# Edge attributes of a graph network brought in feature by edge instead of turned on TensorE

## The chip, the cores and the metric

The kernel runs on one core of one Trainium2 chip. The metric is the device time of one execution, in microseconds (us), on random inputs of fixed shapes.

## The reference

Three layers of a relational graph network on 6250 nodes of 256 features and 100000 edges, sorted by their target node. Each edge has a source, a target, one of three types and 32 attributes. The result is added to the input and normalised.

```python
ew = edge_attr @ edge_w + edge_b                     # (100000, 256)
inv_cnt[i] = 1 / max(edges of type i per target, 1)
for l in range(3):
    msg = relu(x[src] * ew)
    out = x @ roots[l] + biases[l]
    for i in range(3):
        h = segment_sum(msg * (edge_type == i)[:, None], dst) * inv_cnt[i][:, None]
        out = out + h @ weights[l, i]
    x = x + relu(out)
return layernorm(x_input + x)
```

## The kernel before

The edges are cut into 782 tiles of 128, and four tiles make a group, 196 of them (the last has two tiles). In each of the three layers all tiles are worked through two by two. Such a pair is a step, q = 0 to 390. Every engine has its own written-out program, a loop over layers and steps in which q says what is issued when; engines meet only at semaphores. The program is one long straight line behind a check of the input (`both`, `fast`), with a general way beside it that these inputs do not take.

What a pair of tiles needs, engine by engine:

- GpSimd (POOL) issues a `gather` for each tile (line 692, an indirect DMA at line 700): 128 rows of x by the tile's sources, into one of twelve slots of `xg`. A gather waits until the sums of the tile that had its slot are done (`s_sc`).
- TensorE computes `edge_weights` (line 853): attributes times `edge_w` plus `edge_b`, for two tiles into a bank `pE`, with two of them. The left operand is `at`, 128 partitions by 512 edges, three slots (`TR`). Its partitions 0 to 31 hold the attributes' high part, 32 to 63 the low part that was left by rounding, and 64 and up are ones; so one product has both parts and the bias.
- VectorE multiplies the gathered rows by the edge weights in place (line 1300), adds earlier sums to the accumulator `acc` (`add_sums`, line 1138), and makes the matrices `S` that select target and type (line 1097).
- ScalarE applies the ReLU in place (line 791), and in layer 0 makes the one-hot matrices `oh_a` for counting (line 812).
- TensorE sums the messages by target and type, `collect` (line 888, matmuls at line 911), and in layer 0 the counts (line 903).
- When all edges of a block of 128 nodes are summed, the block is mixed: x is turned (`turn_x`), four products with the weights (`mix`, line 961), and VectorE forms the new x in five operations. The blocks start at steps that `plan` works out, six to twelve steps apart.

The part around the change is how `at` comes about. In layer 0, for each group g:

- SP issues `load_attr(g)`: 4 x 128 edges of 32 attributes each, edge by partition, 64 KB, into the slot g % 3 of `hs`, columns 32 to 63 of each tile.
- ScalarE's `high(g)` (line 745) writes the rounded attributes beside them, columns 0 to 31.
- VectorE's `split(g)` (line 1012) subtracts these from the raw ones in place: what is left is the low part.
- TensorE's `attr_turn(g)` (line 846) turns four tiles of 128 edges by 64 columns into the bank `pT`. This bank is shared with `turn_x`.
- ScalarE's `attr_copy(g)` (line 753) copies `pT` to `at`. It waits for the turn, for the edge products that still read the slot (`s_e`), and for the slot's store (`s_ao`).
- SP's `keep_attr(g)` stores the 64 x 512 values of `at` to DRAM (`attr_t`, 128 KB). In layers 1 and 2 SP only loads them back (`reload_attr`).

The places in the steps: SP issues the load of group q/2 + 4 and right behind it the store of group q/2, at even q. ScalarE copies group (q+2)/2 and rounds group (q+6)/2 at even q, after the ReLU. At odd q VectorE splits group (q+6)/2 and TensorE turns group (q+3)/2. SP's load of group g waits until group g - 3 has been turned:

```python
if g >= 3:
    eng.wait_ge(s_tr, g - 2)
```

SP's queue also carries the loads and stores of blocks, in order with the rest. A table `brow` of the first target of each tile, read into VectorE's registers at line 1274, lies in a buffer of its own.

## Time and profile before

| | |
|---|---|
| median of 3 timed runs | 2969.16 us (2966.05 to 2969.5) |
| the profiled execution, first to last instruction | 3581.6 us |
| TensorE: matmuls, weight loads | busy 79%, 73% |
| VectorE, ScalarE, GpSimd | busy 60%, 36%, 62% |
| DMA | 465.42 MB, mean 130 GB/s |

The profiled execution has no time of its own besides its span; what lies around the span is not shown. It is 612 us longer than the timed median. Busy is the time in which an engine had an instruction running; waits for semaphores, register loads and branches are not in it. The chain that ended last is followed back from the last instruction, and the page gives its shares of the span: TensorE 59%, waits for nothing that is shown 17%, VectorE 9%, ScalarE 4%. Within TensorE's share the sums (line 911) have 29%, the edge products (line 867) 14%, the mixes (line 961) 12% and the turns of the attributes (line 846) 2%.

### The profile page before, as it was taken

The numbers are of one execution on the slowest core, as the hardware profiler recorded it, in microseconds if no ns is written. First come the engines' busy times: TensorE is split into PE (matmuls) and PEld (weight loads), VectorE is DVE, ScalarE is ACT, GpSimd is POOL, SyncE is SP. The second block draws the span as 40 slices with busy tenths as digits, with TensorE's granted clock in tenths as the row PEclk, the third lists the DMA queues.
The fourth block names the chain that finished last, engine by engine and source line by source line (L and its number), as shares of the span: only waits on it lengthen the run. The fifth ranks groups of instructions, "written<-read, shape, count | busy, mean of one in ns | idle before, by whom it ended". The sixth has DMA issues, their size and how long they took to land.

```text
span 3581.6 us, 59909 instructions
## 1 busy us (share of the span) xinstructions
PE 2843.8 (79%) x18436; PEld 2613.2 (73%) x18436; DVE 2148.4 (60%) x6028; ACT 1289.4 (36%) x2738; POOL 2224.3 (62%) x2364
## 2 busy tenths in 40 slices
PE   6888888888888877787777877777777777787777
PEld 6777777777777777777777777767777777776776
DVE  5666666666666555555555555555556656665665
ACT  5555555555555322222222222222222222222222
POOL 6666666666666566666666666656666666666664
PEclk9999999999999888888898889988888888899898
DMA  6554555555455444444444444444444444444443
GB/s 148 135 137 132 137 135 138 136 137 137 131 137 145 133 120 127 125 130 127 126 127 127 134 124 127 131 127 132 126 124 128 125 127 131 125 130 124 128 128 99
DMA packets 334989, 465.42 MB, mean 130 GB/s; under 512 B 158995, under 2 KB 221646, under 8 KB 334670
## 3 DMA queue, kind: packets, MB, share of 16 engines
q0 software_dynamic: 112608, 307.65, 30.1%
q1 hardware_dynamic: 221244, 153.70, 15.6%
q8 instruction: 156, 2.56, 0.3%
q14 instruction: 163, 1.34, 0.1%
q10 hardware_dynamic: 818, 0.18, 0.0%
HBM read 403.94 MB, written 57.36 MB: 129 GB/s over the span
## 4 chain that ended last, share of the span: by engine, by line
PE 59%; issue 17%; DVE 9%; another core or an unknown queue 8%; ACT 4%; DVEq 2%; DMA 0%; ACTq 0%
PE bank L911 29%; PE bank L867 14%; PE bank L961 12%; DVE acc L1138 4%; PE bank L846 2%; DVE xg L1300 1%; ACT oh_a L812 1%; DVE t L1155 1%; ACT at L753 1%; DVEq L1274 1%; PE bank L936 1%; DVEq L1138 1%; ACT xg L791 1%; DVE S L1097 1%
## 5 line engine op out<-in xcount | busy, mean ns | idle before, releaser
L700 POOL DMA_INDIRECT xg<-x,idx x1540 | 1457.0, 946 | 870.6 <-issue 351.7
L911 PE MATMUL bank<-S,xg 128*128 128x96 f32 x9384 | 1450.5, 304 | 360.3 <-issue 176.3
L911 PEld LDWEIGHTS bank<-S,xg 128*128 128x128 f32 x9384 | 1313.6, 216 | 429.2 <-issue 385.4
L791 ACT ACTIVATE xg<-xg 128x512 f32<-128x512 f32 x1170 | 736.7, 630 | 2102.3 <-DVE xg L1300 1193.8
L1300 DVE TENSOR_TENSOR xg<-xg,bank 128x512 f32<-128x512 f32 x1170 | 800.8, 684 | 691.0 <-remote 329.4
L1138 DVE TENSOR_TENSOR acc<-acc,bank 128x192 f32 x2346 | 816.7, 348 | 570.0 <-PE bank L911 343.0
L867 PE MATMUL bank<-wsb,at 128*128 128x256 f32 x4692 | 985.7, 337 | 213.6 <-issue 123.3
L700 POOL DMA_INDIRECT xg<-in_x_dram,idx x782 | 742.2, 949 | 454.2 <-PE bank L911 211.2
L867 PEld LDWEIGHTS bank<-wsb,at 128*128 128x128 f32 x4692 | 749.3, 214 | 297.6 <-issue 195.9
L961 PE MATMUL bank<-W,acc 128*128 128x256 f32 (+1 forms) x1764 | 515.9, 415 | 7.2 <-issue 6.4
L961 PEld LDWEIGHTS bank<-W,acc 128*128 128x128 f32 (+1 forms) x1764 | 386.9, 258 | 17.3 <-issue 12.1
L1097 DVE TENSOR_TENSOR S<-bank,kr 128x384 f32<-128x384 f32 x588 | 323.2, 550 | 0.8 <-issue 0.7
L812 ACT ACTIVATE oh_a<-iota,lo 128x128 bf16<-128x128 bf16 x782 | 266.2, 389 | 3.5 <-PE bank L911 3.4
L1155 DVE SCALAR_TENSOR_TENSOR t<-bank,inv,t 128x256 f32<-128x256 f32 (+1 forms) x441 | 209.2, 474 | 17.6 <-remote 10.1
L961 PE MATMUL bank<-W,xT 128*128 128x256 f32 (+1 forms) x588 | 200.2, 472 | 0.9 <-issue 0.8
L846 PE MATMUL bank<-ident,hs 128*64 128x128 f32 x782 | 131.3, 295 | 32.5 <-issue 19.2
L961 PEld LDWEIGHTS bank<-W,xT 128*128 128x128 f32 (+1 forms) x588 | 127.9, 238 | 17.3 <-issue 3.0
L903 PE MATMUL bank<-oh_b,oh_a 128*128 128x12 bf16 x782 | 81.2, 175 | 68.2 <-issue 62.5
L753 ACT ACTIVATE at<-bank 64x512 fp32r<-64x512 f32 x196 | 113.3, 578 | 44.1 <-remote 25.8
L1251 DVE TENSOR_TENSOR cnt<-cnt,bank 128x12 f32<-128x12 f32 x391 | 60.7, 155 | 104.7 <-remote 97.0
L903 PEld LDWEIGHTS bank<-oh_b,oh_a 128*128 128x128 bf16 x782 | 52.6, 107 | 95.5 <-issue 75.3
L846 PEld LDWEIGHTS bank<-ident,hs 128*64 128x64 f32 x782 | 93.2, 128 | 39.4 <-issue 35.1
(75 smaller groups left out, 789.7 us busy)
## 6 DMA issues: line engine op xcount, KB each, us to landing
at<-attr_t SPq DMA_DIRECT2D x390, 128.0 KB
attr_t<-at SPq DMA_DIRECT2D x195, 128.0 KB
xg<-x,idx POOLq DMA_INDIRECT x1540
xg<-in_x_dram,idx POOLq DMA_INDIRECT x782
hs<-in_edge_attr_dram SPq DMA_DIRECT2D x194, 64.0 KB
x<-t SPq DMA_DIRECT2D x96, 128.0 KB
xblk<-x SPq DMA_DIRECT2D x96, 128.0 KB
y<-t SPq DMA_DIRECT2D x94, 128.0 KB
```

The lines of the kernel that those rows point to most:

```text
L700: eng.indirect_dma_start(out=xg[:, n % XR, :], out_offset=None, in_=rows_in, in_offset=bass.IndirectOffsetOnAxis(ap=rows_at, axis=0)).then ...
L753: eng.activation(at[0:64, g % TR, 0:w], pT[0:64, 0:w], ACT.Copy).then_inc(s_atc, 1)
L791: eng.activation(v, v, ACT.Relu).then_inc(s_r, 1)
L812: eng.activation(oh_a[:, j % AR, :], iota[:, 1:129], ACT.Sign, bias=lo[:, tile(j):tile(j) + 1]).then_inc(s_oh, 1)
L846: last = eng.transpose(pT[0:64, 128 * i:128 * i + 128], hs[:, g % 3, i, :], ident[:, :])
L867: last = eng.matmul(pE[Q % 2][:, 256 * i:256 * i + 256], at[:, sl, c:c + 128], wsb[:, p, :], start=(p == 0), stop=(p == 1))
L911: last = eng.matmul(sums_bank(l, q, i)[:, 192 * i + 96 * h:192 * i + 96 * h + 96], xg[:, n % XR, 128 * h:128 * h + 128], S[:, slot(l, 2 * ...
L961: last = eng.matmul(o, a, W[:, 2 * (r % 4) + h, :], start=(h == 0), stop=(h == 1))
L1097: eng.tensor_tensor(S[:, at4:at4 + w, :], steps_of[:, 1:WK + 1].unsqueeze(1).to_broadcast([128, w, WK]), kr[:, c:c + w].unsqueeze(2).to_br ...
L1138: eng.tensor_tensor(a, a, sums_bank(l, q, i)[:, 192 * i:192 * i + 192] .rearrange("p (h w) -> p h w", h=2), ALU.add).then_inc(s_acc, 1)
L1155: return eng.scalar_tensor_tensor(tt, products(k, m), inv[0:n, 3 * blocks[k] + r:3 * blocks[k] + r + 1], tt, ALU.mult, ALU.add)
L1300: eng.tensor_tensor(v, v, pE[Q % 2][:, :].rearrange("p (i d) -> p i d", i=2), ALU.mult).then_inc(s_m, 1)
```

## The change

The host hands over a further array, `attr_2`: the attributes feature by edge, 32 rows, written twice one above the other, so 64 x 100096 values. SP loads 64 x 512 of it for a group, 128 KB, into one of two slots of `hs` (`HR2`). ScalarE copies all 64 partitions with rounding straight to `at`, and VectorE replaces partitions 32 to 63 of `at` by the raw values less the rounded ones. TensorE takes no part, and `attr_turn` and `attr_copy` are gone. The store to DRAM and the layers 1 and 2 stay as they are. The steps of the remaining work move: ScalarE does group (q+4)/2 at even q, and VectorE group (q+3)/2 at odd q. SP's load of group g waits for the split of group g - 2, and its store of group g for that group's split. `brow` moves to the partitions 64 to 127 of `hs`.

```diff
+    HR2 = 2
-    BR = 196
+    BR = 392
-        hs = sb("hs", [128, 3, 4, 64])
+        hs = sb("hs", [128, HR2, 512])
-        brow = sb("brow", [128, BR], I32)
+        brow = hs[64:128, :, :].rearrange("p a b -> p (a b)")[:, 0:BR].bitcast(I32)
...
             def load_attr(g):
-                if g >= 3:
-                    eng.wait_ge(s_tr, g - 2)
-                a, n = 128 * head_tile(order[g]), tiles_of(g) - (g == short)
...
-                eng.dma_start(hs[:, g % 3, 0:n, 32:64], edge_attr[a:a + 128 * n, :]
-                              .rearrange("(j p) d -> p j d", p=128)).then_inc(s_an[g % 3], 16)
+                if g >= HR2:
+                    eng.wait_ge(s_lo, g - HR2 + 1)
+                a, w = 128 * head_tile(order[g]), 128 * tiles_of(g)
+                eng.dma_start(hs[0:64, g % HR2, 0:w], attr_2[:, a:a + w]).then_inc(s_an[g % HR2], 16)
 
             def keep_attr(g):
                 w = 128 * tiles_of(g)
-                eng.wait_ge(s_atc, g + 1)
+                eng.wait_ge(s_lo, g + 1)
                 eng.dma_start(attr_t[g, :, 0:w], at[0:64, g % TR, 0:w].bitcast(F32)).then_inc(s_ao[g % TR], 16)
...
             load_attr(1)
-            load_attr(2)
...
-                            if 3 <= q // 2 + 4 < NG:
+                            if HR2 <= q // 2 + 4 < NG:
                                 load_attr(q // 2 + 4)
...
             def high(g):
 
-                eng.wait_ge(s_an[g % 3], attrs(g))
-                eng.activation(hs[:, g % 3, :, 0:32].bitcast(F32R), hs[:, g % 3, :, 32:64], ACT.Copy).then_inc(s_hi, 1)
-
-            def attr_copy(g):
                 w = 128 * tiles_of(g)
-                eng.wait_ge(s_tr, g + 1)
+                eng.wait_ge(s_an[g % HR2], 16 * (g // HR2 + 1))
                 if g >= TR:
                     eng.wait_ge(s_e, 2 * (g - TR + 1))
                     eng.wait_ge(s_ao[g % TR], 16 * (g // TR))
-                eng.activation(at[0:64, g % TR, 0:w], pT[0:64, 0:w], ACT.Copy).then_inc(s_atc, 1)
+                eng.activation(at[0:64, g % TR, 0:w], hs[0:64, g % HR2, 0:w], ACT.Copy).then_inc(s_hi, 1)
...
-                        if l == 0 and q % 2 == 0 and 1 <= (q + 2) // 2 < NG:
-                            attr_copy((q + 2) // 2)
+                        if l == 0 and q % 2 == 0 and 1 <= (q + 4) // 2 < NG:
+                            high((q + 4) // 2)
...
-                        if l == 0 and q % 2 == 0 and 1 <= (q + 6) // 2 < NG:
-                            high((q + 6) // 2)
...
-                        if l == 0 and q % 2 and 1 <= (q + 3) // 2 < NG:
-                            attr_turn((q + 3) // 2)
...
             def split(g):
 
-                raw, high = hs[:, g % 3, :, 32:64], hs[:, g % 3, :, 0:32]
+                w = 128 * tiles_of(g)
                 eng.wait_ge(s_hi, g + 1)
-                eng.tensor_tensor(raw, raw, high, ALU.subtract).then_inc(s_lo, 1)
+                eng.tensor_tensor(at[32:64, g % TR, 0:w], hs[32:64, g % HR2, 0:w],
+                                  at[32:64, g % TR, 0:w].bitcast(F32), ALU.subtract).then_inc(s_lo, 1)
...
-                        if l == 0 and q % 2 and 1 <= (q + 6) // 2 < NG:
-                            split((q + 6) // 2)
+                        if l == 0 and q % 2 and 1 <= (q + 3) // 2 < NG:
+                            split((q + 3) // 2)
```

How the change stands in the engines' programs, at one place of layer 0 each. SP's queue, before (`s_tr` is the turn, `s_atc` the copy out of the bank, `s_rd` a block's last operation on VectorE):

```order
L562 DMA hs<-in_edge_attr_dram 128x4x32 [waits s_tr]
L568 DMA attr_t<-at 64x512 [waits s_atc]
L562 DMA hs<-in_edge_attr_dram 128x4x32 [waits s_tr]
L568 DMA attr_t<-at 64x512 [waits s_atc]
L562 DMA hs<-in_edge_attr_dram 128x4x32 [waits s_tr]
L568 DMA attr_t<-at 64x512 [waits s_atc]
L580 DMA xblk<-in_x_dram 128x256 [waits s_rd]
```

and in the change, where `s_lo` is the split:

```order
L554 DMA hs<-in_attr_dram 64x512 [waits s_lo]
L559 DMA attr_t<-at 64x512 [waits s_lo]
L554 DMA hs<-in_attr_dram 64x512 [waits s_lo]
L559 DMA attr_t<-at 64x512 [waits s_lo]
L554 DMA hs<-in_attr_dram 64x512 [waits s_lo]
L559 DMA attr_t<-at 64x512 [waits s_lo]
L571 DMA xblk<-in_x_dram 128x256 [waits s_rd]
```

The order of SP's transfers is the same; the load and the store both wait for VectorE's split now.

ScalarE, before (`s_ao0` is the landing of a store to `attr_t`, `s_an` of a load of attributes, `s_m` the multiplication):

```order
L791 ACTIVATE xg<-xg 128x512 [waits s_m]
L812 ACTIVATE oh_a<-iota,lo 128x128 [waits s_sc] x2
L791 ACTIVATE xg<-xg 128x512 [waits s_m]
L753 ACTIVATE at<-bank 64x512 [waits s_ao0,s_e,s_tr]
L745 ACTIVATE hs<-hs 128x4x32 [waits s_an2]
L812 ACTIVATE oh_a<-iota,lo 128x128 [waits s_sc] x2
L791 ACTIVATE xg<-xg 128x512 [waits s_m]
L812 ACTIVATE oh_a<-iota,lo 128x128 [waits s_sc] x2
```

and in the change (line 775 is the ReLU, 794 the one-hots):

```order
L775 ACTIVATE xg<-xg 128x512 [waits s_m]
L794 ACTIVATE oh_a<-iota,lo 128x128 [waits s_sc] x2
L775 ACTIVATE xg<-xg 128x512 [waits s_m]
L738 ACTIVATE at<-hs 64x512 [waits s_ao0,s_e,s_an0]
L794 ACTIVATE oh_a<-iota,lo 128x128 [waits s_sc] x2
L775 ACTIVATE xg<-xg 128x512 [waits s_m]
L794 ACTIVATE oh_a<-iota,lo 128x128 [waits s_sc] x2
```

Two operations for a group have become one, which waits for the landed load and the landed store together.

TensorE around the turn of a block of x (line 936 before, 904 in the change), before:

```order
L936 MATMUL bank<-ident,xblk 128x128 x2
L867 MATMUL bank<-wsb,at 128x256 x4
L903 MATMUL bank<-oh_b,oh_a 128x12 x2
L911 MATMUL bank<-S,xg 128x96 x4
L846 MATMUL bank<-ident,hs 64x128 x4
L867 MATMUL bank<-wsb,at 128x256 x4
L903 MATMUL bank<-oh_b,oh_a 128x12 x2
L911 MATMUL bank<-S,xg 128x96 x4
L961 MATMUL bank<-W,xT 128x256 x2
```

and in the change:

```order
L904 MATMUL bank<-ident,xblk 128x128 x2
L838 MATMUL bank<-wsb,at 128x256 x4
L874 MATMUL bank<-oh_b,oh_a 128x12 x2
L882 MATMUL bank<-S,xg 128x96 x4
L838 MATMUL bank<-wsb,at 128x256 x4
L874 MATMUL bank<-oh_b,oh_a 128x12 x2
L882 MATMUL bank<-S,xg 128x96 x4
L927 MATMUL bank<-W,xT 128x256 x2
```

The turns of the attributes (line 846) are gone, and nothing stands in their place.

## Rows read from the trace of the kernel before

**Rows 1.** Spans by core: span, mean granted clock of TensorE

```profile
core 0: 3581.6 us, clock 0.896
```

**Rows 2.** Groups by line: names, count | busy us, mean ns | idle before, releasers

```profile
L700 POOL DMA_INDIRECT xg<-x,idx x1540 | 1457.0, 946 | 870.6 <-issue 351.7 <-PE bank L911 291.8 <-remote 227.2
```

**Rows 3.** Waits of POOL: us in total, times, longest us

```profile
POOL xg L700 <- issue: 527.0, 1722, 0.6
POOL xg L700 <- PE bank L911: 505.4, 436, 10.0
POOL xg L700 <- remote: 302.9, 186, 2.0
```

**Rows 4.** Timeline of POOL: start us, us, engine, line, operation [idle before, releaser]

```profile
4.73 1.10 POOL L700 DMA_INDIRECT xg<-in_x_dram,idx  x1 [0.97 <-DMA idx<-in_src_t_dram]
...
22.46 0.95 POOL L700 DMA_INDIRECT xg<-in_x_dram,idx  x1 [2.55 <-PE bank L911]
...
1211.05 0.94 POOL L700 DMA_INDIRECT xg<-y,idx  x1 [1.84 <-remote]
...
1217.30 0.95 POOL L700 DMA_INDIRECT xg<-y,idx  x1 [0.30 <-issue]
1228.27 0.94 POOL L700 DMA_INDIRECT xg<-x,idx  x1 [10.02 <-PE bank L911]
...
2405.89 0.94 POOL L700 DMA_INDIRECT xg<-x,idx  x1 [8.76 <-PE bank L911]
...
3561.22 0.95 POOL L700 DMA_INDIRECT xg<-x,idx  x1 [0.30 <-issue]
```

**Rows 5.** Layers 0, 1: us, busy us of PE, PEld, DVE, ACT, POOL, clock, DMA share

```profile
20.00:1200.00 1180.00, 981.71 (x7138) 891.00 (x7137) 750.12 (x2470) 675.16 (x1676) 730.23 (x770) 0.93 0.51 137
1240.00:2395.00 1155.00, 904.94 (x5486) 839.73 (x5486) 654.84 (x1597) 294.71 (x483) 729.26 (x773) 0.87 0.44 128
```

**Rows 6.** Timeline of TensorE's weight loads, layer 0

```profile
1168.35 0.59 PEld L867 LDWEIGHTS bank<-wsb,at 128*128 128x128 f32 x4
...
1169.92 0.94 PEld L961 LDWEIGHTS bank<-W,acc 128*128 128x128 f32 x4
...
1176.73 0.44 PEld L846 LDWEIGHTS bank<-ident,hs 128*64 128x64 f32 x4
```

**Rows 7.** Groups by line that the change takes away or replaces

```profile
L846 PE MATMUL bank<-ident,hs 128*64 128x128 f32 x782 | 131.3, 295 | 32.5 <-issue 19.2 <-DVE hs L1012 7.0 <-ACT xT L799 6.3
...
L753 ACT ACTIVATE at<-bank 64x512 fp32r<-64x512 f32 x196 | 113.3, 578 | 44.1 <-remote 25.8 <-PE bank L846 14.2 <-issue 2.3
...
L745 ACT ACTIVATE hs<-hs 128x128 fp32r<-128x128 f32 x196 | 58.0, 296 | 0.0
L1012 DVE TENSOR_TENSOR hs<-hs 128x128 f32<-128x128 f32 x196 | 55.7, 285 | 4.4 <-ACT hs L745 3.4 <-issue 1.1
```

**Rows 8.** Groups by line nearest to the new operations

```profile
L1300 DVE TENSOR_TENSOR xg<-xg,bank 128x512 f32<-128x512 f32 x1170 | 800.8, 684 | 691.0 <-remote 329.4 <-PE bank L867 247.9 <-issue 110.1
...
L791 ACT ACTIVATE xg<-xg 128x512 f32<-128x512 f32 x1170 | 736.7, 630 | 2102.3 <-DVE xg L1300 1193.8 <-issue 907.3
```

**Rows 9.** Timeline of VectorE: two steps of layer 0 without a wait

```profile
714.70 0.69 DVE L1300 TENSOR_TENSOR xg<-xg,bank 128x512 f32<-128x512 f32 x1 [0.38 <-issue]
...
718.75 0.68 DVE L1300 TENSOR_TENSOR xg<-xg,bank 128x512 f32<-128x512 f32 x1
```

**Rows 10.** Timeline of SP's queue: the load and the store of one group

```profile
701.62 0.37 SPq L562 DMA_DIRECT2D hs<-in_edge_attr_dram  x1
702.04 0.51 SPq L568 DMA_DIRECT2D attr_t<-at  x1
```

**Rows 11.** DMA issues: name, engine, count, KB, us from issue to landing

```profile
acc<-in_dst_t_dram SPq DMA_DIRECT2D x1, 391.0 KB, 3.9
...
idx<-in_src_t_dram ACTq DMA_DIRECT2D x1, 4.0 KB, 2.0
idx<-in_src_t_dram ACTq DMA_DIRECT2D x1, 2.0 KB, 3.2
```

45 lines of the change are left out of this document (13 added, 32 removed).

## The prediction

> **What bounds the kernel now.** I first read the span against the timed runs. The profiled execution lasted 3581.6 us [rows 1], the timed runs 2969.16 us in the median: the profiled one is 612 us, or 21%, longer, so its times cannot be added up as they stand. What can be used of it is how long each thing takes when nothing disturbs it. TensorE has the largest busy share of the page, and the chain that ended last runs mostly through it; taken alone, that says that removing its work pays.
>
> The waits of POOL say otherwise. POOL issues 2346 gathers, each 0.946 us [rows 2]. In 1722 of the gaps between them it waited for nothing the profile shows, 0.306 us each (527.0 / 1722) [rows 3]; five gaps in a row put the pitch at (1217.30 - 1211.05) / 5 = 1.25 us [rows 4]. That is a floor for the program. Add it up: first gather at 4.7 us; 2345 pitches of 1.25 us, 2931; the 13th gather, the first behind the branch, waits 2.55 - 0.30 = 2.2 us more; the two turns from layer to layer 10.02 - 0.30 = 9.7 and 8.76 - 0.30 = 8.5 us; from the last gather to the end 3581.6 - 3561.2 = 20.4 us [rows 1, 4]. Sum: 2977 us. The timed median is 8 us (0.3%) below it; a pitch of 1.2467 us, 0.946 + 0.30 with the rounding of the rows, would give it exactly. A second count from the same views: the waits for TensorE and for landings are 505.4 + 302.9 us in 622 gaps; with 0.306 us left in each of them, 3581.6 - 808.3 + 190.3 = 2964 us, and 2984 with the 20 us of the branch and the two turns put back [rows 1, 3]. So the profiled execution is long because of interruptions that the timed ones do not have, and the timed kernel is POOL issuing gathers with hardly a hole. Two tiles are one step, so a step is 2.50 us and a group of four tiles, which one attribute load serves, 5.0 us.
>
> The other engines have to stay under that pace. Layer 0 and layer 1 do, at nearly one pace, 1180 us for 770 gathers against 1155 us for 773, although TensorE is busy 982 us in the one and 905 us in the other [rows 5].
>
> **The change part by part.**
> *TensorE loses the turns.* Four transposes a group, 0.44 us of weight loads at the full clock [rows 6]; times 196 groups that is 86 us (all of the group row: 131.3 us busy [rows 7]). A step of the edge products, counts and sums takes 1169.92 - 1168.35 = 1.57 us, half a turn 0.22, and a block's four mixes of 0.9 us every 8 steps 0.45: 2.24 us, and 2.39 us where blocks follow every 6 steps [rows 6]. Both are under 2.50, which hides them. Worth: nothing to at most 86 us. I take nothing, because the floor above already accounts for the whole time.
>
> *ScalarE* did a copy out of PSUM, 578 ns, and a rounding, 296 ns [rows 7]. It now does one copy of 64x512 from SBUF; the nearest row is the 128x512 ReLU at 630 ns [rows 8]. Saved: 0.24 us a group, 48 us in all, of an engine busy 675 of 1180 us [rows 5]. Hidden, worth nothing.
>
> *VectorE* subtracted 128x128 in 285 ns [rows 7] and now 32x512: time goes by elements along a partition, so the 128x512 row counts, 684 ns [rows 8]. That is 0.40 us more a group, 78 us in all. Two steps without a wait, with block work and the register load in them, take 718.75 - 714.70 = 4.05 us [rows 9]; plus 0.40 is 4.45, still under 5.0. Cost nothing, with 0.55 us of cover left; before it had 0.95.
>
> *SyncE and the two rings.* Loads grow from 64 to 128 KB, 12.8 MB in all. The DMA engines' share is 0.51 in layer 0 and 0.44 in layer 1 [rows 5], so that is no bound. But the order of waits changes. Before, SP's load for group g+4 waited for the turn of group g+1, and the store of group g behind it came five steps ahead of the copy that overwrites its slot. Now the load of g+4 waits for the split of g+2, at VectorE's step 2g+1; the store of g queues behind it; and ScalarE's copy for g+3, at its step 2g+2, needs that store landed. Behind it wait the one-hots of the next step, the next ReLU, and VectorE's split of g+3, which again frees SP. One round of this loop: the store starts 702.04 - 701.62 = 0.42 us behind the load [rows 10]; the landing L; the copy 0.63; the split 0.68; and 0.2 us for the four hops (estimate: 0.03 to 0.1 each by the starts in the timelines). The trace shows no landing of such a store. The nearest rows are 2.0 and 3.2 us for 4 and 2 KB and 3.9 us for 391 KB [rows 11]; 128 KB lies nearest the small ones, on the line from 2.0 to 3.9 at 2.6 us. The round is 1.93 + L = 4.5 us against 5.0: it fits. At the ends it is 3.9 and 5.8 us. I take 4.5 us, cost nothing. ScalarE will be seen waiting at this copy all the same, up to about 1 us a group, since it reaches it some 2 us after the split; it waited 44.1 us there in all before [rows 7]. The Trainium skill ("DMA: Bandwidth & Descriptors", Anatomy of one DMA) gives 2.0 us plus bytes by 436 GB/s for a DMA that GpSimd issues; by it L would be 2.3 and the round 4.2 us, and the sum stays.
>
> *The start.* No turn stands ahead of the first sums; they may come 1 us earlier, and the 13th gather with them [rows 4]. Bounds 0 and 2.2 us; taken 1. The branch behind the check stays.
>
> Sum: 2969.2 - 1 = **2968 us**. The ring of twelve gathers is six steps deep, 15 us, so a late copy now and then does not reach POOL. (A measurement of this kernel can tell about 0.2%, 6 us, from no change.)
>
> **Rivals.**
> *TensorE shares the bound in layer 0.* For it: at the granted 0.93 [rows 5] the dense step is 2.39 / 0.93 = 2.57 us, over 2.50. Layer 0 takes 1.532 us a gather and layer 1 1.494: times 782 that is 30 us more. If half goes to the turns (the counts are the rest), 15 us come back: 2953 us. Against it: without interruptions TensorE has no reason to sit at the lower clock, and the floor leaves no such 30 us. Should the timed pitch be well under 1.25, all 86 us could count, 2883 us; I hold that for very unlikely.
>
> *The store loop becomes the bound, slower.* It decides from L = 3.07 us on, where a round passes 5.0. At the 3.2 us of the 2 KB row it is 5.13 us, 0.13 x 196 = 25 us: 2993 us; at 3.9 us it would be 0.83 x 196 = 163 us. For it: the store now runs behind a load of 128 KB on the same queue, among gathers, and VectorE has half the cover that it had. Against it: the larger of these landings are from the start, where many loads are issued together.
>
> *POOL is held up by the new subtraction, slower.* The split reads two SBUF operands, as the old one did, and 0.40 us longer. If POOL stood still meanwhile, 78 us would be added: 3046 us. Against it: POOL's gathers take 0.946 us in layers 1 and 2 [rows 2], which have no split, and 0.95 us in layer 0 as well [rows 4]. The Trainium skill ("SBUF — State Buffer", SBUF: two separate sides) says that a VectorE operation with two SBUF inputs and a GpSimd operation that reads SBUF lock each other out of shared ports.
>
> *The change does not do what it says*: the turns are gone from TensorE's program, so I give this none.
>
> **How the numbers follow.** POOL paces as before 0.57; TensorE's relief shows 0.20; store loop 0.18; ports 0.05. Faster by over 0.2% 0.20, within 0.57, slower 0.23. The likeliest case gives 2968 us. The range must leave out no more than 0.2: down to 2948 (the relief at 20 us), up to 2998 (the loop at 3.2 us of landing, and a little), leaving out the 86 us, L above 3.2 us and the ports.
>
> **What would show it.** In the changed profile: the pitch of POOL's gathers again 1.25 us; TensorE's busy time in layer 0 down by 90 to 130 us while the layer keeps its length; the split at 0.68 to 0.70 us; ScalarE's copy near 0.63 us, with idle time before it, released by a landing, over the 44.1 us of before but under 200. A median under 2955 us would prove me wrong on TensorE. One over 2980 us with ScalarE idle over 1.5 us before each copy would say that the store loop binds; with gathers longer than 0.95 us, the ports.

## The result, and the profile after

| | before | changed |
|---|---|---|
| median of 4 timed runs each | 2967.91 us | 3016.82 us |
| lowest to highest | 2966.05 to 2969.5 | 3013.34 to 3022.49 |
| the profiled execution, span | | 3011.4 us |

The changed kernel is slower by 48.9 us, ratio 1.017, 95% interval 1.0156 to 1.0184. The forecast was 2968 us with a range up to 2998.

The page of the changed kernel (span; busy time by engine; TensorE's granted clock; the chain that ended last, by engine and by line):

```profile
span 3011.4 us, 57947 instructions
...
PE 2562.5 (85%) x17654; PEld 2355.0 (78%) x17654; DVE 2222.4 (74%) x6028; ACT 1247.4 (41%) x2542; POOL 2236.1 (74%) x2363
...
PEclk9899899999999999999999999999999999999999
...
PE 32%; DMA 30%; POOL 12%; issue 10%; DVE 8%; ACT 4%; SPq 3%; DVEq 0%; ACTq 0%; POOLq 0%
PE bank L882 17%; DMA attr_t<-at 16%; DMA xg<-x,idx 14%; POOL xg L689 12%; PE bank L927 8%; PE bank L838 7%; DVE at L976 3%; ACT at L738 3%; SPq L554 2%; DVE acc L1103 2%; DVE xg L1265 1%; DVE t L1120 1%; PE bank L904 0%; DMA at<-attr_t 0%; PE bank L874 0%
```

The granted clock stands at nine tenths or more in all but three of the 40 slices, and its mean is 0.952: 2.4 GHz for some nine tenths of the time, 1.2 GHz for the rest. TensorE is the busiest engine. The chain has an entry that the chain before did not show: the store `attr_t<-at`, 16% of the whole span, although it exists in one layer of three.

Groups of instructions (busy us, mean ns of one | idle us before them and what ended it):

```profile
L689 POOL DMA_INDIRECT xg<-in_x_dram,idx x782 | 753.4, 963 | 278.6 <-issue 163.5
...
L976 DVE TENSOR_TENSOR at<-hs,at 32x512 fp32r<-32x512 f32 x196 | 133.6, 682 | 172.4 <-ACT at L738 171.4
L738 ACT ACTIVATE at<-hs 64x512 fp32r<-64x512 f32 x196 | 123.3, 629 | 308.5 <-DMA attr_t<-at 278.1
```

ScalarE's copy is 629 ns and VectorE's split 682 ns, as forecast. The third row is where the forecast fell: 278.1 us of ScalarE's idle time end with the landing of a store. The first one holds the second surprise, 963 ns for a gather in layer 0.

The waits (engine, line, waited for: us in total, times, longest):

```profile
POOL xg L689 <- issue: 491.0, 1611, 0.5
ACT at L738 <- DMA attr_t<-at: 278.1, 174, 5.0
...
POOL xg L689 <- PE bank L882: 266.5, 734, 3.8
...
DVE at L976 <- ACT at L738: 171.4, 176, 4.2
```

The time goes on from ScalarE to VectorE (171.4 us). For POOL the waits of a profiled execution of the kernel before that took 2963.9 us (`before_again`, below) stand beside them:

```profile
POOL xg L700 <- issue: 498.8, 1635, 0.5
...
POOL xg L700 <- PE bank L911: 220.1, 710, 2.7
```

A stretch of layer 0 and one of layer 1 (busy us and count of PE, PEld, DVE, ACT, POOL; clock, DMA share, GB/s), first of the changed kernel, then of `before_again`:

```profile
20.00:980.00 960.00, 809.18 (x6031) 756.86 (x6030) 781.99 (x2337) 604.97 (x1406) 703.27 (x731) 0.94 0.59 171
1060.00:2000.00 940.00, 813.99 (x5410) 737.04 (x5409) 642.39 (x1572) 287.35 (x475) 710.90 (x753) 0.97 0.53 154
```

```profile
20.00:980.00 960.00, 891.11 (x7123) 845.30 (x7123) 746.04 (x2464) 666.00 (x1671) 725.62 (x765) 0.98 0.63 167
1010.00:1980.00 970.00, 834.98 (x5543) 753.06 (x5543) 659.59 (x1612) 293.91 (x486) 733.79 (x776) 0.97 0.53 153
```

In layer 1 the kernels go at one pace: 940 / 753 = 1.248 us a gather against 970 / 776 = 1.250. The loss is in layer 0: 731 gathers in 960 us against 765, that is 1.3133 us against 1.2549, and 0.0584 x 782 = 46 of the 49 us. The stretches are of one length but hold different amounts of work, so for busy times the whole of layer 0 is compared, from the first of its 782 gathers to the last (changed kernel, then `before_again`):

```profile
5.05:1035.60 1030.55, 860.05 (x6385) 803.65 (x6385) 839.04 (x2503) 649.65 (x1499) 753.35 (x782) 0.94 0.60 172
```

```profile
4.29:987.10 982.81, 903.27 (x7198) 855.53 (x7198) 760.96 (x2511) 682.71 (x1700) 743.41 (x782) 0.98 0.63 167
```

The layer is 48 us longer. TensorE had its relief (860 us busy against 903) and it bought nothing.

One thing on reading the times. The profile shown ahead of the prediction (span 3581.6 us) was no accident of one execution. The later half of the experiments ran on chips on which the kernel before takes 3584 to 3587 us run after run, as in the trace of [rows 3, 5]. Such traces have waits that end by "remote", a releaser that the profile can't name (302.9 us of POOL's in [rows 3]; the 2964-us trace has none above). They also hold fewer of the marks with which a DMA reports its landing, 3.8 for a gather in the mean where `before_again` has 15.8; so "remote" may be no more than marks that are missing, and landings are timed below from traces of the 2966-us chips alone. Why those chips are slower is open. Where an experiment ran there, the text says so, and its time is set only beside that of the kernel before on the same chip.

### The profile page after: what moved, and what is told of

The parts are those of the page before. It is cut to its first block, busy times and chain, and to the rows that moved or that the text cites. A ratio compares the mean times of both kernels' runs of the same rounds, so it can differ in the third digit from the quotient of the medians.

```text
span 3011.4 us, 57947 instructions
## 1 busy us (share of the span) xinstructions
PE 2562.5 (85%) x17654; PEld 2355.0 (78%) x17654; DVE 2222.4 (74%) x6028; ACT 1247.4 (41%) x2542; POOL 2236.1 (74%) x2363
## 4 chain that ended last, share of the span: by engine, by line
PE 32%; DMA 30%; POOL 12%; issue 10%; DVE 8%; ACT 4%; SPq 3%; DVEq 0%; ACTq 0%; POOLq 0%
PE bank L882 17%; DMA attr_t<-at 16%; DMA xg<-x,idx 14%; POOL xg L689 12%; PE bank L927 8%; PE bank L838 7%; DVE at L976 3%; ACT at L738 3%; SPq L554 2%; DVE acc L1103 2%; DVE xg L1265 1%; DVE t L1120 1%; PE bank L904 0%; DMA at<-attr_t 0%; PE bank L874 0%
## 5 line engine op out<-in xcount | busy, mean ns | idle before, releaser
L882 PE MATMUL bank<-S,xg 128*128 128x96 f32 x9384 | 1344.9, 289 | 126.9 <-DVE acc L1103 87.1
L882 PEld LDWEIGHTS bank<-S,xg 128*128 128x128 f32 x9384 | 1207.2, 201 | 201.1 <-ACT xg L775 154.5
L838 PE MATMUL bank<-wsb,at 128*128 128x256 f32 x4692 | 925.3, 321 | 149.2 <-DVE xg L1265 133.1
L838 PEld LDWEIGHTS bank<-wsb,at 128*128 128x128 f32 x4692 | 696.8, 199 | 220.4 <-issue 106.0
L976 DVE TENSOR_TENSOR at<-hs,at 32x512 fp32r<-32x512 f32 x196 | 133.6, 682 | 172.4 <-ACT at L738 171.4
L738 ACT ACTIVATE at<-hs 64x512 fp32r<-64x512 f32 x196 | 123.3, 629 | 308.5 <-DMA attr_t<-at 278.1
L927 PE MATMUL bank<-W,xT 128*128 128x256 f32 (+1 forms) x588 | 168.1, 412 | 0.0
L927 PEld LDWEIGHTS bank<-W,xT 128*128 128x128 f32 (+1 forms) x588 | 110.7, 206 | 10.5
L747 ACT ACTIVATE acc<-zcol 128x768 f32<-128x768 f32 (+1 forms) x98 | 81.2, 831 | 10.7 <-PE bank L927 10.7
L1132 DVE TENSOR_TENSOR t<-bank,bias 128x256 f32<-128x256 f32 (+1 forms) x147 | 61.1, 416 | 5.2 <-PE bank L927 4.7
```

The costliest lines, as they stand in the source:

```text
L738: eng.activation(at[0:64, g % TR, 0:w], hs[0:64, g % HR2, 0:w], ACT.Copy).then_inc(s_hi, 1)
L838: last = eng.matmul(pE[Q % 2][:, 256 * i:256 * i + 256], at[:, sl, c:c + 128], wsb[:, p, :], start=(p == 0), stop=(p == 1))
L882: last = eng.matmul(sums_bank(l, q, i)[:, 192 * i + 96 * h:192 * i + 96 * h + 96], xg[:, n % XR, 128 * h:128 * h + 128], S[:, slot(l, 2 * ...
L927: last = eng.matmul(o, a, W[:, 2 * (r % 4) + h, :], start=(h == 0), stop=(h == 1))
L976: eng.tensor_tensor(at[32:64, g % TR, 0:w], hs[32:64, g % HR2, 0:w], at[32:64, g % TR, 0:w].bitcast(F32), ALU.subtract).then_inc(s_lo, 1)
```

## The experiments

My theory after the result had two parts: **the store's round**, split, load, store, landing, copy, split, longer than the 5.0 us of a group; and, once the first runs were in, **the ports**: gathers drawn out by the longer split. The rivals were VectorE at its limit, and DMA traffic. The ports are a name for one thing that the runs show: a gather gets longer when it starts inside a VectorE operation that reads two operands from SBUF.

A table carries the readings from the chips on which the kernel before took 2966.3 and 2966.1 us (2967.9 beside the changed kernel). The pace is 960 us by the number of gathers in the stretch from 20 to 980 us, and the gather's mean is from the group rows of the same stretch (shown below, kernel by kernel). "Longer" is (mean - 950 ns) x 782, "holes" is what is left of (pace - 1.2549) x 782; one gather more or less in the count is 1.3 us, one ns 0.8 us. The two columns say where POOL's time went. They are not two prices that could be saved one by one: while POOL waits for the store's round anyway, a longer gather only fills a part of that wait.

| kernel | gathers | mean ns | pace us | longer us | holes us | sum us | timed over before us |
|---|---|---|---|---|---|---|---|
| before_again | 765 | 950 | 1.2549 | 0 | 0 | 0 | 0 |
| one_turn | 763 | 949 | 1.2582 | -1 | 3 | 3 | 1 |
| late_store | 757 | 949 | 1.2682 | -1 | 11 | 10 | 8 |
| changed | 731 | 963 | 1.3133 | 10 | 36 | 46 | 49 |
| store_first | 754 | 969 | 1.2732 | 15 | -1 | 14 | 17 |
| store_same_wait | 739 | 991 | 1.2991 | 32 | 3 | 35 | 31 |
| store_first_dve | 749 | 975 | 1.2817 | 20 | 1 | 21 | 22 |
| store_first_half | 765 | 951 | 1.2549 | 1 | -1 | 0 | 3 |
| store_first_wide | 751 | 971 | 1.2783 | 16 | 2 | 18 | 16 |

**before_again**, the kernel before, unchanged.

> The kernel before, unchanged, profiled once more: is its span of 3581.6 us, 612 us over the timed runs, a property of the kernel or of that one execution? If POOL paces it as summed up, an undisturbed profile spans 2960 to 2975 us, with POOL's gathers 1.25 us apart nearly everywhere.

Measured 2965.61 us, span 2963.9, clock 0.964. Its gathers in layer 0:

```profile
L700 POOL DMA_INDIRECT xg<-in_x_dram,idx x765 | 726.5, 950 | 234.5 <-issue 162.1 <-PE bank L911 72.4
```

It is the yardstick of the table. It has no long waits in POOL's row (2.7 us at most), and its pace is the floor of 1.25 us a gather that the prediction built from gaps [rows 3, 4].

**one_turn**: the kernel before with one of four turns, so without most of what the change takes from TensorE.

```diff
-                for i in range(tiles_of(g)):
+                for i in range(tiles_of(g) if g == 0 else 1):
```

> The kernel before with one of the four transposes of a group (from the second group on), so three quarters of the turn's TensorE work are left out (the attributes of three tiles of four are then stale ones), everything else as it was. If POOL paces the kernel: 2964 to 2970 us. If TensorE shares the bound in layer 0: up to 65 us less (three quarters of 86), 2903 to 2955 us.

Measured 2967.0 us, ratio 1.0002 (0.9993 to 1.0012).

```profile
L700 POOL DMA_INDIRECT xg<-in_x_dram,idx x763 | 724.4, 949 | 235.6 <-issue 167.0 <-PE bank L911 68.6
```

TensorE's relief alone is worth nothing: the interval bars a gain of over 0.1%. POOL starts its gathers at the same pace.

**store_first**: the changed kernel with SP's store ahead of its load.

```diff
-                            if HR2 <= q // 2 + 4 < NG:
-                                load_attr(q // 2 + 4)
                             if 0 <= q // 2 < NG:
                                 keep_attr(q // 2)
+                            if HR2 <= q // 2 + 4 < NG:
+                                load_attr(q // 2 + 4)
```

> The changed kernel with SyncE's store of group q/2 issued ahead of the load of group q/2+4, so that the store no longer stands behind the load's wait for the split of group q/2+2 and goes out two steps earlier. Store loop theory: ScalarE's idle time before its copy (309 us) falls below 60 us, POOL issues without a hole in layer 0 too, 2960 to 2975 us. If VectorE's longer subtraction or the DMA traffic is what costs, nothing changes: 3010 to 3020 us.

Measured 2982.89 us, ratio 1.0059 (1.0042 to 1.0076). ScalarE's wait for the store in layer 0 is next to nothing:

```profile
ACT at L738 <- DMA attr_t<-at: 6.7, 4, 2.9
```

```profile
L689 POOL DMA_INDIRECT xg<-in_x_dram,idx x754 | 730.9, 969 | 229.8 <-issue 156.6 <-PE bank L882 73.2
```

The load of group g+4 waits for the split of g+2 as before, but what follows it on the queue is now the store of g+1, not of g. Each store goes out a group earlier, the round is open, and 32 of the 49 us are back with two lines exchanged, although the store takes no less to land (3.25 us in the median) and the DMA share is as high as in before_again, 0.62 against 0.63. DMA traffic is out as the cause. I had expected 2975 us at most: 17 us stay though ScalarE no longer waits. The gathers show where: 969 ns.

**store_same_wait**: store first again, but held until the split for which the load waits. It keeps the round and takes only the load from in front of the store.

```diff
                             if 0 <= q // 2 < NG:
+                                eng.wait_ge(s_lo, min(q // 2 + 3, NG))
                                 keep_attr(q // 2)
```

> The changed kernel with the store ahead of the load, but made to wait for the split of group q/2+2 all the same. Only the 0.5 us behind the load's issue, and the load's bytes ahead of it, are taken from the loop. Store loop theory: the round of 5.0 us becomes 4.2 to 4.5 us and the time 2970 to 2990 us. If what counts is how early the store goes relative to its split, whatever stands before it: about 3015 us. VectorE or traffic: 3015 us.

Measured 2996.82 us, ratio 1.0099 (1.0082 to 1.0116).

```profile
L690 POOL DMA_INDIRECT xg<-in_x_dram,idx x739 | 732.3, 991 | 228.2 <-issue 151.4 <-PE bank L883 76.8
```

ScalarE's wait for the store is 45.7 us in the stretch, against 259.1 us in the changed kernel, and POOL's holes are gone. The time is over store_first's and over my 2990 us all the same, and it is the gathers: 991 ns, the longest of all. That was the pointer to the second part of the theory. In this order 100 gathers start 0.05 to 0.5 us into a split, against 56 in store_first and 40 in the changed kernel, and every one of them is long.

**late_store**: the kernel before, its short split and its 64 KB loads, with each store held until a later split.

```diff
-                            if 0 <= q // 2 < NG:
-                                keep_attr(q // 2)
+                            if 0 <= q // 2 - 1 < NG - 1:
+                                eng.wait_ge(s_lo, min(q // 2 + 4, NG))
+                                keep_attr(q // 2 - 1)
...
```

> The kernel before, turns and all, with one thing changed: the store of a group is held until VectorE has split the group four further on, which leaves it one step before the copy that overwrites its slot, as in the changed kernel. Store loop theory: 2990 to 3030 us, with ScalarE waiting for a landing before the copy out of the bank. If the new subtraction, the larger loads or the missing turns are the cause: 2968 us.

Measured 2974.19 us, ratio 1.0025 (1.0015 to 1.0036), far under what I expected.

```profile
ACT at L756 <- DMA attr_t<-at: 54.1, 99, 3.2
```

```profile
L703 POOL DMA_INDIRECT xg<-in_x_dram,idx x757 | 718.5, 949 | 241.9 <-issue 156.9 <-PE bank L914 85.0
```

ScalarE waits for the store 99 times, 54.1 us in the stretch, and 8 us reach the end. A miss of mine: I had looked at how late one store is. What counts is the length of the closed round. Here it is shorter than in the changed kernel, which also has the load's 0.52 us and a longer split in it, and whose store takes 3.05 us to land in the median against 2.49 here.

**store_first_dve**: store_first with one subtraction of VectorE's more for each group, 128x256, two SBUF operands.

```diff
+                if g >= 2:
+                    eng.wait_ge(s_pad, g - 2)
+                    eng.tensor_tensor(pad[:, :], wsb[:, 0, :].bitcast(F32), wsb[:, 1, :].bitcast(F32),
+                                      ALU.subtract).then_inc(s_pad, 1)
...
```

> The changed kernel with the store ahead of the load (2983 us), and VectorE given one more subtraction of 128x256 to a spare tile in each group of layer 0, some 0.35 us. If the 17 us left over the kernel before are VectorE at its limit: 40 to 65 us more, 3023 to 3048 us. If VectorE still has the half microsecond of cover that the prediction gave it, or the larger loads are the cause: 2983 to 2990 us.

Measured 2988.07 us, ratio 1.0072 (1.0055 to 1.0089).

```profile
L691 POOL DMA_INDIRECT xg<-in_x_dram,idx x749 | 730.4, 975 | 231.0 <-issue 155.7 <-PE bank L884 75.3
```

VectorE is busy 878 of the 960 us here, against 826 in store_first, and it costs 5 us. VectorE is not what limits layer 0; the gathers are again a little longer, 975 ns, and 36 of the lengthened ones end behind the new subtraction, which also reads two SBUF operands.

**store_first_half**: store_first with a split over half of the columns, 0.42 us long (half of the low parts are left out of what is computed).

```diff
-                w = 128 * tiles_of(g)
+                w = 64 * tiles_of(g)
```

> The changed kernel with the store ahead of the load, and the subtraction done for half of a group's columns (the low parts of the other half stay as rounded values): 0.26 us less of VectorE per group, the DMA traffic as it was. VectorE at its limit: 2966 to 2972 us, the time of the kernel before. Traffic: 2983 us.

Measured 2969.0 us, ratio 1.0011 (1.0001 to 1.0021).

```profile
L689 POOL DMA_INDIRECT xg<-in_x_dram,idx x765 | 727.4, 951 | 233.4 <-issue 169.7 <-PE bank L882 63.7
```

The gathers are back at 951 ns, and all but 3 us of the loss are gone. By its time alone this run speaks for VectorE at its limit as much as for the ports; the runs before and behind it, with VectorE's load changed and the split as it was, part the two.

**store_first_wide**: store_first, with VectorE's register loads halved in number, which gives VectorE time and touches neither split nor DMA of the attributes.

```diff
-                        if 0 <= q < NP and q % 2 == 0:
-                            w, c = min(4, NT - 2 * q), tile(2 * q)
+                        if 0 <= q < NP and q % 4 == 0:
+                            w = min(8, NT - 2 * q)
...
```

> The changed kernel with the store ahead of the load, and VectorE reading eight first targets at once into its registers every four steps, where it read four every two steps (the host lays the table out in the order of the work). The same result with half as many register loads, some 0.25 us less of VectorE per group. VectorE at its limit: 2967 to 2975 us. It cannot come below the kernel before, if POOL paces that. Traffic: 2983 us.

Measured 2982.25 us, ratio 1.005 (1.0033 to 1.0067).

No change against store_first. With store_first_dve this rules out VectorE at its limit as the cause.

**What a long gather looks like.** The timeline of store_first (start us, us, engine, line, operation):

```profile
514.13 0.68 DVE L976 TENSOR_TENSOR at<-hs,at 32x512 fp32r<-32x512 f32 x1
...
514.41 1.23 POOL L689 DMA_INDIRECT xg<-in_x_dram,idx  x1 [0.30 <-PE bank L882]
515.59 0.68 DVE L1265 TENSOR_TENSOR xg<-xg,bank 128x512 f32<-128x512 f32 x1
515.95 0.95 POOL L689 DMA_INDIRECT xg<-in_x_dram,idx  x1 [0.30 <-issue]
...
518.46 0.95 POOL L689 DMA_INDIRECT xg<-in_x_dram,idx  x1 [0.30 <-issue]
...
518.87 0.68 DVE L976 TENSOR_TENSOR at<-hs,at 32x512 fp32r<-32x512 f32 x1
```

The split runs from 514.13 to 514.81. The gather that starts in it, at 514.41, takes 1.23 us and ends at 515.64, 0.83 us behind the split; the next one starts 0.31 us later, so POOL's whole row has moved by 0.28 us. The split at 518.87 starts 0.41 us after its gather did, and that gather takes 0.95 us: a split that starts in a running gather does not hold it.

Between them stands the best control, in the same trace. The multiplication at 515.59 is as long as the split but reads one of its operands from a bank of PSUM, and the gather that starts 0.36 us into it takes 0.95 us. Counted over layer 0 of store_first: of 45 gathers that start 0.1 to 0.5 us into a split all are over 1 us long, 1.17 in the mean; of 163 that start so into a multiplication none is. So it is not VectorE's being busy that holds them.

**psum_const**: store_first, with the split's second operand read from a bank of PSUM. Length, count and place stay; one SBUF operand is gone.

```diff
                 eng.tensor_tensor(at[32:64, g % TR, 0:w], hs[32:64, g % HR2, 0:w],
-                                  at[32:64, g % TR, 0:w].bitcast(F32), ALU.subtract).then_inc(s_lo, 1)
+                                  bank[5][32:64, 0:w], ALU.subtract).then_inc(s_lo, 1)
...
```

> The changed kernel with SP's store ahead of its load (as in store_first), and VectorE's split takes its second operand from a PSUM bank that holds a constant instead of from the rounded copy in SBUF: the same 512 columns and 32 partitions, but one SBUF operand instead of two. So the low parts of the attributes are left out of what is computed. Theory (the gathers are lengthened by a split with two SBUF operands): layer 0's gathers come back from 969 ns to 947 to 952 ns and the time from 2983 to 2964 to 2970 us. Rival (VectorE's or ScalarE's busy time, or the DMA traffic of the host-laid attributes, makes the rest of the loss): gathers stay near 969 ns and the time stays at 2980 to 2986 us.

This run and those below were made on the chips of the other kind. The kernel before took 3584.43 us here, psum_const 3585.77, ratio 1.0011 (0.9998 to 1.0024).

```profile
L689 POOL DMA_INDIRECT xg<-in_x_dram,idx x626 | 592.3, 946 | 369.1 <-PE bank L882 208.3 <-issue 142.2 <-remote 18.6
```

The gather's length does not depend on the kind of chip (0.95 us for the kernel before in [rows 4] and 950 ns in before_again), and it is back: 946 ns, with splits as long as ever, 0.68 us. It was run twice more:

> psum_const again, on a chip on which the kernel before takes 2966 us (the low parts of the attributes are left out of what is computed). The gathers' length is known from the first look: 946 ns in layer 0. Theory (the 17 us of store_first over before are its lengthened gathers): 2964 to 2970 us. Rival (they are something else that the new split or the host's layout brings): 2980 to 2986 us with gathers of 946 ns all the same.

> psum_const once more (the low parts of the attributes are left out of what is computed). On a chip where before takes 2966 us: 2964 to 2970 us if the lengthened gathers are the 17 us that store_first is over before, 2980 to 2986 us if they are something else. On one where before takes 3584 us: 3585 to 3589 us, as twice before, 8 to 12 us under the changed kernel.

Measured 3586.72 us against 3584.02, ratio 1.0012 (1.0002 to 1.0021), and 3588.62 against 3584.56, 1.0009 (0.9999 to 1.0018); gathers of 948 and 949 ns. No chip of the first kind was met. The timeline of the second run shows the counterpart of the long gather:

```profile
503.89 0.68 DVE L976 TENSOR_TENSOR at<-hs,bank 32x512 fp32r<-32x512 f32 x1
503.95 0.95 POOL L689 DMA_INDIRECT xg<-in_x_dram,idx  x1 [0.30 <-issue]
...
522.64 0.68 DVE L976 TENSOR_TENSOR at<-hs,bank 32x512 fp32r<-32x512 f32 x1
523.00 0.95 POOL L689 DMA_INDIRECT xg<-in_x_dram,idx  x1 [0.30 <-issue]
```

Gathers that start 0.06 and 0.36 us into a split take 0.95 us. In this run 118 gathers start 0.1 to 0.5 us into a split and none is over 0.96 us; in the changed kernel on such a chip (`after_again`, below) it is 110, and all are over 1 us. So the second SBUF operand is shown as the cause of the long gathers. That their length is also all that store_first had over before, on the chips where before takes 2966 us, rests on the sums in the table; this kernel did not run there. Nor did any run keep the store's round and take away the long gathers alone, so how much of the 49 us the long gathers cost beside the round is not shown.

**half_load**: the changed kernel in its own order, but with loads of 32 partitions, 64 KB (the low parts are left out of what is computed).

```diff
-                eng.dma_start(hs[0:64, g % HR2, 0:w], attr_2[:, a:a + w]).then_inc(s_an[g % HR2], 16)
+                eng.dma_start(hs[0:32, g % HR2, 0:w], attr_2[0:32, a:a + w]).then_inc(s_an[g % HR2], 16)
...
```

> The changed kernel in its own order (load ahead of store), but the load brings 32 partitions (64 KB) instead of 64 (128 KB); the other 32 rows hold ones set once, so the low parts of the attributes are left out of what is computed. The split still has two SBUF operands. Theory (35 us of the loss are the closed round of store, copy and split, with the store landing behind the load): the store lands some 0.3 to 0.6 us sooner than its median of 3.05 us, the holes in POOL's row shrink to under 15 us, and the time falls to 2985 to 3005 us; the gathers stay long (963 to 975 ns). Rival (the number of queue entries, not the load's bytes, delays the store): unchanged at 3012 to 3020 us.

> half_load again, on a chip on which the kernel before takes 2966 us (the low parts of the attributes are left out of what is computed). Theory (the store lands late because 128 KB of load stand ahead of it): ScalarE's wait for attr_t under 150 us in all (278 in the changed kernel) and 2990 to 3008 us. Rival (the queue entry, not its bytes, delays the store): 3012 to 3020 us. On a chip where before takes 3584 us: only the wait is read.

Measured 3592.19 us, ratio 1.0022 (1.0013 to 1.0032), and 3589.33, ratio 1.0018 (1.0008 to 1.0027). For a comparison the changed kernel itself was run on such a chip:

> The changed kernel as it is. On a chip where before takes 2966 us: 3012 to 3020 us again, nothing new. On one where before takes 3584 us, POOL waits some 220 us in each layer for the others, so a part of the change's cost falls into time in which POOL waits anyway: the store's round and the long gathers should cost less than 49 us there. Theory (half_load took away a part of the store's delay, psum_const the store's order and the long gathers): 3592 to 3620 us, above half_load's 3589 to 3592. Rival (neither of the two things matters): 3584 to 3592 us, the same as half_load and psum_const.

Measured 3597.59 us against 3586.58, ratio 1.0032 (1.002 to 1.0045). ScalarE's wait for the store from 20 to 980 us, first in the changed kernel, then in half_load:

```profile
ACT at L738 <- DMA attr_t<-at: 156.1, 115, 3.5
```

```profile
ACT at L739 <- DMA attr_t<-at: 89.0, 88, 2.2
```

The change costs 11 us where POOL has other waits to hide it in, against 49. With half of the load ahead of the store ScalarE's wait falls from 156.1 to 89.0 us (92.2 in the second run), in step with the theory (where marks of a landing are missing, a wait can be left out of such a sum), but the intervals of the times overlap and settle nothing. Gathers are 965 and 957 ns in the two runs of half_load and 971 in the changed kernel: they are long here too.

**psum_high**: an attempt at a good version. The whole computation, store first, and the rounded high part of rows 32 to 63 goes to PSUM by a second copy of ScalarE's, where the split reads it. The turn of a block of x waits for the splits, since it uses the same bank.

```diff
-                eng.activation(at[0:64, g % TR, 0:w], hs[0:64, g % HR2, 0:w], ACT.Copy).then_inc(s_hi, 1)
+                eng.activation(at[0:32, g % TR, 0:w], hs[0:32, g % HR2, 0:w], ACT.Copy).then_inc(s_hi, 1)
...
+                eng.activation(pT[32:64, 0:w].bitcast(F32R), hs[32:64, g % HR2, 0:w], ACT.Copy).then_inc(s_hi, 1)
...
```

> The whole computation, with SP's store ahead of its load: ScalarE writes the rounded high part of rows 32 to 63 into the PSUM bank that the old turns used, and VectorE's split reads it there, so that it has one SBUF operand. ScalarE has two copies for each group instead of one (some 0.6 us more in a round of two steps), and TensorE's turn of a block waits for the splits before it. Theory: with gathers back at 947 to 952 ns and no store in the way, 2964 to 2972 us, no faster than the kernel before (2966), because POOL's pitch paces both. Rival (TensorE's relief is worth something once the two costs of the change are gone): under 2960 us. If the additional copy brings the store loop back: over 2975 us with ScalarE waiting for the store or the load in layer 0.

> psum_high again, on a chip on which the kernel before takes 2966 us: the whole computation, split with one SBUF operand, two copies of ScalarE. Theory: 2964 to 2972 us if the additional copy has slack, no faster than before since POOL's pitch paces both. If the round with two copies (some 0.6 us longer than store_first's) is over 5.0 us: 2975 to 3000 us with ScalarE waiting for attr_t or VectorE for ScalarE. Rival (TensorE's relief is worth something once the costs are gone): under 2960 us.

Measured 3609.2 us, ratio 1.0078 (1.0057 to 1.0098), and 3610.82, ratio 1.0075 (1.0059 to 1.0092); 25 us over before, and more than the changed kernel's 11 on such chips. The gathers are short, 945 and 949 ns.

POOL waits more for TensorE, 228.2 us against 204.1 in the second run of psum_const, and TensorE's turn of a block of x (line 912) waits for a split now and then (waits of the second run, 20 to 980 us):

```profile
POOL xg L689 <- PE bank L888: 228.2, 161, 3.0
...
PE bank L912 <- DVE at L984: 24.0, 7, 5.7
```

The two differences, 24.1 and 24.0 us, are of one size; that the one makes the other is my reading, no run parts them. Whether this kernel would tie on the other chips is open. None of my versions beats the kernel before.

**pool_pad and pool_pad_three**: the kernel before with one tiny memset of POOL's after each gather of layer 0, and with three.

```diff
+                if l == 0:
+                    if j:
+                        eng.wait_ge(s_pad, j)
+                    eng.memset(pad[:, :], 0.0).then_inc(s_pad, 1)
```

> The kernel before with one tiny memset of POOL's own (128 partitions, one column) after each of layer 0's 782 gathers, nothing else changed. Theory (POOL's pitch of 1.25 us paces layer 0): the pitch grows by the memset and its dispatch, some 0.06 to 0.2 us, and the time by the same 782 times: 3010 to 3120 us, or at any rate by 782 times what the pitch grows by. Rival (TensorE and VectorE pace layer 0, POOL only waits for them): under 2975 us, with the added work inside POOL's idle time.

> The kernel before with three memsets of POOL's own (128 partitions, 32 columns) after each of layer 0's 782 gathers. Three of some 0.12 us and their dispatch don't fit into the 0.30 us between two gathers. Theory (POOL's pitch of 1.25 us paces layer 0): the pitch grows by 0.15 to 0.4 us and the time by 782 times what the pitch grows by, 120 to 310 us. Rival (TensorE and VectorE pace layer 0): under 2980 us, the addition inside POOL's idle time.

One memset: 3587.47 us, ratio 1.0012 (1.0001 to 1.0022). I had expected that it adds 40 us or more. POOL's timeline shows why it tells nothing:

```profile
409.95 0.95 POOL L702 DMA_INDIRECT xg<-in_x_dram,idx  x1 [0.19 <-issue]
410.90 0.11 POOL L708 MEMSET pad<- 128x1 f32 x1
411.20 0.95 POOL L702 DMA_INDIRECT xg<-in_x_dram,idx  x1 [0.19 <-issue]
```

It lies within the 0.30 us that stand between two gathers anyway, and the pitch is 1.25 us still. Three memsets make it 1.37 us:

```profile
405.44 0.95 POOL L702 DMA_INDIRECT xg<-in_x_dram,idx  x1 [0.16 <-issue]
406.39 0.26 POOL L709 MEMSET pad<- 128x32 f32 x3
406.81 0.95 POOL L702 DMA_INDIRECT xg<-in_x_dram,idx  x1 [0.16 <-issue]
```

That came to 3597.07 us, ratio 1.0033 (1.0018 to 1.0049): 13 us, not 0.12 x 782 = 94. On chips of this kind POOL waits for others often enough to take in most of it, so there POOL is not the sole pace. On the first kind this test was not made; that POOL paces there rests on one_turn, on the missing holes, and on longer gathers coming out one for one in the time wherever the store's round is open.

## Why the prediction was wrong, point by point

- **POOL paces the kernel, a step is 2.50 us: right**, on the chips of the timed runs. before_again has 1.250 us a gather in layer 1 and 1.2549 in layer 0. The prediction took the long profile for interruptions that the timed runs do not have. That held for the timed runs, but 3584 us is how some chips run this kernel.
- **TensorE's relief is worth nothing: right** (one_turn, +1 us). The rival at 2953 us is out. The sign that I had set for it did not come, though: TensorE's busy time in layer 0 fell by 43 us (903 to 860), not by 90 to 130, and the layer did not keep its length. The 131 us of the turns in [rows 7] are from the long profile, with 295 ns for one; they take 273 ns in before_again, and what else TensorE does then runs at a granted clock of 0.94 against 0.98. Nothing of the forecast hung on that number.
- **ScalarE and VectorE: the durations right, 629 and 682 ns, the cost of VectorE's part wrong.** The cover of 0.55 us was not used up (store_first_dve put 52 us more on VectorE for 5 us). But "cost nothing" left out what the longer split does to POOL.
- **The store loop: the failing step is "the round is 1.93 + L = 4.5 us against 5.0: it fits".** The mechanism and its members were right, and the limit L = 3.07 us nearly so (3.00 by the rows below); L was mis-sized. I took 2.6 us. In the changed kernel's trace the 196 landings have a median of 3.05 and a mean of 3.23 us, and 19 are over 4. The chain of waits shows two rounds in a row:

```profile
498.94 0.69 DVE at L976
...
499.65 0.47 SPq L554
...
500.17 3.21 DMA attr_t<-at
...
503.48 0.64 ACT at L738
...
504.15 0.69 DVE at L976
...
505.37 5.09 DMA attr_t<-at
```

From split to split (498.94 to 504.15) are 5.21 us with a landing of 3.21, so 2.00 + L; the next landing takes 5.09 us. Of the 196 landings 107 take over 3.00 us, and the late ones are not made up, since the next round begins where this one ended. That is the place where the ring of twelve gathers was trusted wrongly: "a late copy now and then does not reach POOL". In POOL's timeline such a streak ends in holes:

```profile
1008.77 0.94 POOL L689 DMA_INDIRECT xg<-in_x_dram,idx  x1 [3.34 <-PE bank L882]
...
1013.04 0.95 POOL L689 DMA_INDIRECT xg<-in_x_dram,idx  x1 [2.08 <-PE bank L882]
```

The mean round of 2.00 + 3.23 = 5.23 us is the pace of the layer, 4 x 1.3133 = 5.25 us for a group, and gives 0.23 x 196 = 45 of the 46 us. So the round by itself accounts for nearly all of the loss; the table's 36 us of holes are smaller because 10 us of longer gathers lie inside the same rounds. The signs set for this rival came too: a median over 2980 us and ScalarE idle 308.5 / 196 = 1.6 us before a copy, where over 1.5 was asked.
- **What to take for L.** The nearest rows were landings at the start [rows 11]. The same store behind 64 KB of load has 2.94 us in the median in before_again, so a median close to 3 could have been had only from a trace of the first kind. The small DMAs of the start were the wrong neighbours for 128 KB among gathers. The Trainium skill ("DMA: Bandwidth & Descriptors", Anatomy of one DMA) makes it 2.3 us by its fit for DMAs that GpSimd issues; here the measurement decides, 3.05 us behind a load and 2.3 in store_same_wait, where nothing is ahead (medians). So its fit is met by a store alone on its queue and is 0.75 us short in this place.
- **The ports: the mechanism right, its price and its chance wrong.** I had 78 us, for POOL standing still during all that the split is longer, and set a chance of 0.05 on it. By the length of the gathers it is 10 us in the changed kernel, inside the round's loss, and up to 32 in another order. Taking it as nothing is the second step that failed: 17 us stay in store_first with the round open. The evidence against it was worth little. A held gather ends 0.82 us after the split's end and is held only if it starts over some 0.05 us into the split; so a split of 0.285 us can draw out the 0.946 us of a gather by 0.285 + 0.82 - 0.05 - 0.946 = 0.11 us at most (my estimate), one of 0.68 us by 0.5. The Trainium skill ("SBUF — State Buffer", SBUF: two separate sides) says that a VectorE operation with two SBUF inputs and a GpSimd operation that reads SBUF shut each other out. With that the trace agrees as far as the gather goes: 1.23 us with two SBUF operands, 0.95 with one, so a gather behaves as such a reader. The other half is not seen here: the 156 splits of store_first that start over 0.1 us into a running gather take 0.68 us as ever.
- **The chances.** Store loop 0.18 and ports 0.05 were rivals, each alone; both came. The loop alone, at the measured 5.23 us, gives 2968 + 45 = 3013 us, past 2998 already. A loop at 90% of its limit, on a duration with no row of its own, should have had more.

## What to carry to other kernels

When a change sets a DMA behind another on one queue and the same queue's next wait depends on its landing, count the closed round, with the landing measured in that place and with its spread, against the period; where the period lies within that spread it will bind, and exchanging two issues may be all it needs. Time taken from an engine that does not pace is worth nothing, while time given to VectorE in an operation with two SBUF operands can lengthen GpSimd's gathers. Look at the mean of the pacing engine's own instruction in each stage, not only at waits. Before building on a profile that is far over the timed runs, get another one.

## What the runs showed of the hardware

- An indirect gather of POOL's that starts inside a VectorE operation with two SBUF operands is held until 0.82 us after that operation's end; alone it takes 0.946 us. In store_first all 56 gathers that start 0.05 to 0.5 us into a split are long; of 148 that start up to 0.8 us before a split or within its first 0.05 us, one is. 74 gathers of layer 0 are long there, by 0.26 us in the mean: 59 end so behind a split, 11 behind the `t<-t,xblk` of a block, which has two SBUF operands too, and 4 behind operations of the program's start, of which some have one; what decides there was not tested. A split is not slowed by a gather that already runs: of 156 that start over 0.1 us into one, none takes over 0.683 us.
- The same operation with one operand in PSUM does not hold a gather: none of 163 in store_first that start into a multiplication of 0.68 us, none of 118 in the second psum_const that start into a split.
- Behind each gather stand 0.30 us in which POOL can do a memset of 0.11 us with the pitch still 1.25 us (pool_pad).
- The same 128 KB store lands after 2.3 us with nothing ahead (store_same_wait), 2.94 behind 64 KB (before_again) and 3.05 to 3.25 behind 128 KB of load on its queue (changed, store_first; medians from the start of the issue).
- On some chips the kernel before takes 3584 us instead of 2966, run after run, with TensorE's granted clock at 0.88 to 0.90 in the mean against 0.96, gathers of the same length, and waits that end by a releaser the profile can't name. What lies behind it was not found.
